# Attention of a fused Mamba, attention and expert layer: short matmul passes joined in pairs, the normalisation of the probabilities shared by VectorE and GpSimd, and the output projection's wait split by batch

## What is computed

```python
x = rmsnorm(hidden_states, ln1_w)                       # (4, 256, 256)
q = (x @ q_w.T).reshape(b, s, 16, 192)[..., :128]        # 16 heads of 128
k = (x @ kv_w.T)[..., :16*128].reshape(b, s, 16, 128)
v = (x @ kv_w.T)[..., 16*128:16*256].reshape(b, s, 16, 128)
scores = einsum('bqnd,bknd->bnqk', q, k) * 192 ** -0.5
scores = where(causal, scores, -1e9)
p = softmax(scores, axis=-1)
attn = einsum('bnqk,bknd->bqnd', p, v).reshape(b, s, 16*128)
hid = hidden_states + attn @ o_w.T
```

## Time and profile before

| | |
|---|---|
| three runs before | 781.72, 781.1, 780.4 us; median 781.1 |
| the profiled execution | 783.59 us |
| its span (first to last instruction) | 781.5 us |
| mean granted TensorE clock | 0.987 |
| busy in the span | PE 744.0 us, PEld 587.5, DVE 574.5, ACT 463.4, POOL 286.6 |
| the attention | from about 266 us to about 550 us of the span |

### The profile page before, as it was taken

One profiled execution on the slowest core, in us unless ns is written; L12 is line 12 of the kernel. 1 busy time (PEld: TensorE's weight loads), 2 busy tenths in 40 slices (PEclk: granted clock), 3 DMA queues, 4 the chain that ended last, 5 costly groups with the idle time before them and its releaser, 6 DMA issues.

```text
span 781.5 us, 12391 instructions
## 1 busy us (share of the span) xinstructions
PE 744.0 (95%) x4164; PEld 587.5 (75%) x4164; DVE 574.5 (74%) x1218; ACT 463.4 (59%) x1022; POOL 286.6 (37%) x181
## 2 busy tenths in 40 slices
PE   7997999999979999999999999999998999999996
PEld 3444455455546899999999999998877888898886
DVE  3699999999898678748775776678665564647376
ACT  4699878878665467727773675476662343425153
POOL 1007989998769711201210211000433231313140
PEclk9998999999999999999999999999999999999999
DMA  8022423333221200000010110001219161515101
GB/s 326 12 75 81 119 97 118 116 103 109 67 77 54 72 28 28 29 28 28 29 55 1 31 50 28 21 21 55 88 53 259 49 179 51 147 50 184 48 0 54
DMA packets 25213, 59.03 MB, mean 76 GB/s; under 512 B 3617, under 2 KB 5153, under 8 KB 25041
## 3 DMA queue, kind: packets, MB, share of 16 engines
q1 hardware_dynamic: 25024, 58.21, 24.3%
q10 hardware_dynamic: 144, 0.26, 0.1%
HBM read 57.21 MB, written 1.25 MB: 75 GB/s over the span
## 4 chain that ended last, share of the span: by engine, by line
PE 58%; DVE 8%; ACT 3%; issue 2%; DMA 1%; DVEq 0%; SPq 0%; ACTq 0%
PE ps L1034 17%; PE ps L1035 17%; PE ps L1036 17%; PE ps L1191 3%; PE ps L549 2%; DVE e_aw L2007 2%; DVE e_sg L1999 1%; ACT e_ah L1853 1%; PE ps L553 1%; DVE e_al L2013 1%; DVE m_ring L903 1%; ACT e_sg L1849 0%; ACT a_p L1343 0%; DVE hid L2018 0%; PE ps L498 0%
## 5 line engine op out<-in xcount | busy, mean ns | idle before, releaser
L549 PE MATMUL ps<-m_ring,ident 128*128 128x512 f32 x256 | 121.7, 604 | 5.6 <-POOL m_ring L406 5.4
L1145 POOL TENSOR_TENSOR a_wl<-raw,a_wh 128x1024 fp32r<-128x1024 f32 (+1 forms) x16 | 32.1, 2008 | 239.4 <-ACT a_wh L1331 239.4
L1668 POOL TENSOR_TENSOR e_wl<-raw,e_wh 128x512 fp32r<-128x512 f32 (+1 forms) x55 | 59.2, 1087 | 154.0 <-ACT e_wh L1804 85.8
L406 POOL TENSOR_TENSOR m_ring<-m_ring,m_c_sb 128x1024 f32<-128x1024 f32 x40 | 94.6, 2373 | 18.3 <-DVE m_ring L903 16.3
L398 POOL TENSOR_TENSOR m_ring<-m_du,m_b_sb 128x1024 f32<-128x1024 f32 x31 | 73.6, 2374 | 59.8 <-DVE m_ring L890 59.8
L549 PEld LDWEIGHTS ps<-m_ring,ident 128*128 128x128 f32 x256 | 47.1, 192 | 50.2 <-issue 37.1
L903 DVE TENSOR_TENSOR_SCAN m_ring<-m_first,ps 128x1024 f32<-128x1024 f32 x32 | 72.8, 2275 | 7.7 <-ACT ps L752 4.2
L1034 PE MATMUL ps<-a_rowsh,e_wh 128*128 128x512 f32 x200 | 78.3, 391 | 0.2 <-ACT e_sg L1849 0.2
L1035 PE MATMUL ps<-a_rowsl,e_wh 128*128 128x512 f32 x200 | 77.9, 389 | 0.0
L1036 PE MATMUL ps<-a_rowsh,e_wl 128*128 128x512 f32 x200 | 77.9, 389 | 0.0
L1343 ACT ACTIVATE a_p<-a_p,a_nmax 128x128 f32<-128x128 f32 (+1 forms) x128 | 57.1, 448 | 29.2 <-DVE a_nmax L1436 27.9
(11 more groups left out here) (221 smaller groups left out, 2144.4 us busy)
## 6 DMA issues: line engine op xcount, KB each, us to landing
raw<-in_expert_w SPq DMA_DIRECT2D x30, 384.0 KB, 3.3
raw<-in_attn_w SPq DMA_DIRECT2D x20, 512.0 KB, 3.3
m_c_sb<-bc SPq DMA_DIRECT2D x40, 256.0 KB, 3.5
m_b_sb<-bc SPq DMA_DIRECT2D x32, 256.0 KB, 4.1
e_wb<-wt SPq DMA_DIRECT2D x18, 256.0 KB, 4.5
e_wb<-wt SPq DMA_DIRECT2D x4, 448.0 KB, 5.8
e_wb<-wt SPq DMA_DIRECT2D x4, 384.0 KB, 4.5
x<-in_x_tok SPq DMA_DIRECT2D x1, 1024.0 KB, 10.2
```

The costliest lines, as they stand in the source:

```text
L406: nc.gpsimd.tensor_tensor(split(slot(n)), split(slot(n)), c_sb[:, k % C_BUFS:k % C_BUFS + 1, :].to_broadcast([P, 2, HALF]), ALU.mult).then ...
L549: nc.tensor.matmul(ps[:, Y_BANK + c, :], ident[:, :], slot(n)[:, c * HALF:(c + 1) * HALF], start=False, stop=False, skip_group_check=True) ...
L1668: nc.gpsimd.tensor_tensor(w[1][:, k, cols], raw[:, k, cols], w[0][:, k, cols].bitcast(F32), ALU.subtract).then_inc(low, 1)
```

## The change

Three things change, and with them two tensors' layouts: the high and low parts of the keys become one tensor `a_k`, those of the transposed probabilities one tensor `a_pT`, so that both parts can stream in one pass.

1. `joined_passes` replaces three passes of 128 columns by one of 128 (low weights by the high streamed part) and one of 256 (high weights by both streamed parts at once). The product with the low streamed part goes to a PSUM block of its own and is added by VectorE: in `maxes` by one more instruction of 128 columns ahead of the others, in `low_o` by one more behind, which waits for the instruction before it (`o_joined`).
2. `normalize` loses its multiplication of 256 columns to GpSimd (a tensor_tensor with the reciprocal broadcast); what stays on VectorE is `one_over`. `turn` waits for both.
3. `outputs(g)` waits for the low parts of each batch in turn instead of for all four.

```diff
@@ Space
-            self.k, self.q, self.rows = (parts(name, [P, 2, T]) for name in ("k", "q", "rows"))
+            self.k = ctx.enter_context(nc.sbuf_tensor("a_k", [P, 2, 2, T], F32R))
+            self.q, self.rows = (parts(name, [P, 2, T]) for name in ("q", "rows"))
...
-            self.pT = parts("pT", [P, 2, 3 * P])
+            self.pT = ctx.enter_context(nc.sbuf_tensor("a_pT", [P, 2, 2, 3 * P], F32R))
@@ new function
+def joined_passes(nc, out, lhs, both, start, stop):
+    lh, ll = lhs
+    nc.tensor.matmul(out[:, 0, :], ll, both[:, 0, :], start=start, stop=False, skip_group_check=True)
+    return nc.tensor.matmul(out, lh, both, start=False, stop=stop, skip_group_check=True)
@@ attention_block, gpsimd
+        def normalize(n, b):
+            pool.wait_ge(rs_done, n + 1)
+            nc.gpsimd.tensor_tensor(p[:, b, P:3 * P], p[:, b, P:3 * P], rs[:, b, 1:2].to_broadcast([P, 2 * P]),
+                                    ALU.mult).then_inc(norm_done, 1)
+
+        def step(g, j, cols):
+            n = g * (GH * BATCH) + j * BATCH
+            for b in range(1, BATCH):
+                normalize(n + b, b)
+            pack(g * GH + (GH + j), j, cols)
+            if not (isinstance(g, int) and g == LAST and j == GH - 1):
+                normalize(n + BATCH, 0)
...
@@ tensor, scores
-            for first, keys, cols in ((t0, P, slice(0, P)), (t0 + P, SEQ, slice(P, 3 * P))):
-                mm = three_passes(nc, bank[:, cols], [x[:, j % 2, first:first + P] for x in q],
-                                  [x[:, j % 2, t0:t0 + keys] for x in k_], first == t0, True)
+            blocks = bank.rearrange("p (a c) -> p a c", c=P)
+            joined_passes(nc, blocks[:, 0:4:3, :], [x[:, j % 2, t0:t0 + P] for x in q],
+                          space.k[:, :, j % 2, t0:t0 + P], True, True)
+            mm = three_passes(nc, bank[:, P:3 * P], [x[:, j % 2, t0 + P:t0 + SEQ] for x in q],
+                              [x[:, j % 2, t0:t0 + SEQ] for x in k_], False, True)
             mm.then_inc(s_ready, 1)
@@ turn
             pe.wait_ge(norm_done, n + 1)
+            pe.wait_ge(first_done, n + 1)
@@ weigh
-            three_passes(nc, bank[:, P:SEQ], vs[1], [x[:, b % 2, 2 * P:3 * P] for x in pT], False,
-                         True).then_inc(o_ready, 1)
+            blocks = bank.rearrange("p (a c) -> p a c", c=P)
+            joined_passes(nc, blocks[:, 1:3, :], vs[1], space.pT[:, :, b % 2, 2 * P:3 * P], False,
+                          True).then_inc(o_ready, 1)
@@ outputs
-            pe.wait_ge(ol_done, g * (GH * BATCH) + GH * BATCH)
             pe.wait_ge(w_done, g * GH + 2 * GH)
             for i in range(TT):
+                if i % 2 == 0:
+                    pe.wait_ge(ol_done, g * (GH * BATCH) + ((GH - 1) * BATCH + i // 2 + 1))
                 pe.wait_ge(r_free, out_unit(g, i) - 1)
@@ vector, maxes
-            nc.vector.memset(rs[:, b, :], 0.0)
-            for t, cols in ((0, slice(0, P)), (1, slice(P, 3 * P))):
-                m = nc.vector.tensor_tensor_reduce(out=p[:, b, cols], in0=ps[:, 2 + b % 2, cols], in1=mask[:, cols],
+            nc.vector.tensor_tensor(p[:, b, 0:P], ps[:, 2 + b % 2, 3 * P:4 * P], mask[:, 0:P], ALU.add
+                                    ).then_inc(masked, 1)
+            for t, cols, more in ((1, slice(P, 3 * P), mask[:, P:3 * P]), (0, slice(0, P), p[:, b, 0:P])):
+                if t == 0:
+
+                    dve.wait_ge(masked, n + 1)
+                    nc.vector.memset(rs[:, b, :], 0.0)
+                m = nc.vector.tensor_tensor_reduce(out=p[:, b, cols], in0=ps[:, 2 + b % 2, cols], in1=more,
@@ normalize, now one_over
             nc.vector.reciprocal(rs[:, b, :], sums[:, b, :]).then_inc(rs_done, 1)
             dve.wait_ge(rs_done, n + 1)
-            for t, cols in ((0, slice(0, P)), (1, slice(P, 3 * P))):
-                m = nc.vector.tensor_scalar(p[:, b, cols], p[:, b, cols], rs[:, b, t:t + 1], None, ALU.mult)
-            m.then_inc(norm_done, 1)
+            nc.vector.tensor_scalar(p[:, b, 0:P], p[:, b, 0:P], rs[:, b, 0:1], None, ALU.mult).then_inc(first_done, 1)
@@ low_o
-                                    ALU.subtract).then_inc(ol_done, 1)
+                                    ALU.subtract).then_inc(o_joined, 1)
+            dve.wait_ge(o_joined, n + 1)
+            late = o[1][:, j, b * SEQ + P:(b + 1) * SEQ]
+            nc.vector.tensor_tensor(late, late.bitcast(F32), ps[:, 6 + b % 2, SEQ:SEQ + P], ALU.add).then_inc(ol_done, 1)
```

More of the change, by code:

```diff
@@ L1048, in attention_block @@
     raw = keep["raw"]
-    w, q, k_, v, p, pT, o = space.w, space.q, space.k, space.v, space.p, space.pT, space.o
+    w, q, v, p, o = space.w, space.q, space.v, space.p, space.o
+    k_, pT = ([x[:, part] for part in range(2)] for x in (space.k, space.pT))
     nmax, sums, rs = (sb(f"a_{n}", [P, 4, 2]) for n in ("nmax", "sums", "rs"))
@@ L1056, in attention_block @@
     rs_done, norm_done = sem("rs_done"), sem("norm_done")
+    masked, o_joined, first_done = sem("masked"), sem("o_joined"), sem("first_done")
     pT_ready, ph_done, pl_done = sem("pT_ready"), sem("ph_done"), sem("pl_done")
@@ L1146, in pack @@
                                     ALU.subtract).then_inc(w_done, 1)
-        with pool.Fori(1, NG) as g:
+        def normalize(n, b):
[9 more added lines that the diff above has]
+                normalize(n + BATCH, 0)
+        normalize(0, 0)
+        for j in range(GH):
+            step(0, j, slice(0, PACK))
+        with pool.Fori(1, LAST) as g:
             for j in range(GH):
-                pack(g * GH + j, j, slice(0, PACK))
+                step(g, j, slice(0, PACK))
         for j in range(GH):
-            pack(NG * GH + j, j, OUT_COLS)
+            step(LAST, j, OUT_COLS)
     def tensor(pe):
@@ L1439, in maxes, with one_over @@
             m.then_inc(max_done, 1)
-        def normalize(n, b):
+        def one_over(n, b):
             dve.wait_ge(exp_done, n + 1)
@@ L1481, in vector @@
             first(s)
-        normalize(0, 0)
+        one_over(0, 0)
         def step(g, j):
@@ L1493, in step @@
             if not units:
-                normalize(n + 1, 1)
+                one_over(n + 1, 1)
                 maxes(n + 2, 2)
@@ L1498, in step @@
                 low_p(n + 1, 1)
-                normalize(n + 2, 2)
-                normalize(n + 3, 3)
+                one_over(n + 2, 2)
+                one_over(n + 3, 3)
                 low_o(n, j, 0)
@@ L1531, in step @@
             low_o(n + 3, j, 3)
-            normalize(n + BATCH, 0)
+            one_over(n + BATCH, 0)
             fill(5)
```

## The result

The changed kernel took 806.9 us (median of 4 runs, 806.1 to 808.09), the kernel before 781.4 (median of 4, 780.4 to 782.23): a ratio of 1.034, interval 1.032 to 1.0361. It is slower, as forecast, but by 25 us and not by 10: the time lies outside the range. It is the time of rival (b).

The account below looks back on a forecast made before the run. Bound twice a step: TensorE 15.26 us, a VectorE-ScalarE chain about 15.16. Chain +0.90, less 0.10 slack and 0.10 shorter weigh 2, gives +0.70 a step; 13 steps 9.1, with the others +10.5: 791.6 us, range 780 to 797.

Parts of the forecast that it names:

- rival (b): GpSimd gets the ports first, VectorE's multiplication waits 0.74 us each time: +1.15 us a step more, 807 us; chance 0.07.
- For batch 2 it helps nothing, since normalize 3 waits for exps 3: VectorE's normalize: losing the 256-column multiplication saves 0 on the chain for batch 2; -0.54 us for batches 1 and 3.
- The slack of 0.10: Chain through VectorE and ScalarE, at weigh 2: it could grow 0.10 us a step before TensorE had to wait.
- the 0.90 of the prediction: Growth of VectorE's chain a step: 0.63 maxes, -0.54 normalize, 0.66 low_o, 0.15 GpSimd's multiplication, +0.90 us.
- `maxes` +0.21: VectorE's maxes: one more addition of 128 columns, +0.21 us, on the chain for batches 0, 2 and 3: +0.63.
- `low_o` 0.67: VectorE's low_o: with the addition behind it 0.67 us instead of 0.34, on the chain for batches 0 and 1: +0.66.
- GpSimd's multiplication: GpSimd's part of normalize: 0.742 us for 256 columns, delaying VectorE's multiplication of batch 3 by 0.15 us.
- The outputs' wait, 0: Start of outputs: TensorE's wait of 0.41 us moves to the second tile, 0 to +0.1 us, not -0.4.
- VectorE's chain, not this, decides when weigh 2 starts: TensorE's turn: probabilities come later, it waits 0.3 us at turn 0 and a like time at turn 2, costing 0.
- Rival (a): TensorE's saving comes through: faster, 778 or 768 us; decided at a chain growth of 0.2 us a step; chance 0.12.
- (c): VectorE's additions are cheaper than the nearest rows or half hidden: growth 0.3 to 0.5 us a step, 783 to 787; chance 0.13.
- (d): No change: the chain's growth and TensorE's saving cancel, 780 to 782.5 us; chance 0.06.

Follow-up runs that it names:

- a1: Changed kernel, but GpSimd's multiplication waits for the end of VectorE's multiplication instead of the reciprocals: 792.1 us.
- a6: Changed kernel, but GpSimd first multiplies two columns of a constant and waits for that, so its 256 columns start later: 790.3 us.
- b1: Kernel before with the split normalisation alone, VectorE's and GpSimd's multiplications both waiting for the reciprocals: 788.3 us.
- b3: Kernel before with the scores' passes joined alone, and the addition in maxes that this needs: 789.2 us.
- a2: Changed kernel with the whole normalisation back on VectorE; joined passes and split outputs' wait stay: 797.3 us.
- b2: Kernel before with the outputs' wait split by batch, alone: 781.2 us, ratio 1.002.
- c6: Scores joined for batch 1, weigh for 2 and 3; GpSimd helps batches 1 and 3, after VectorE; outputs by batch: 776.2 us, 0.9933 of the kernel before.
- a4: Changed kernel with GpSimd's multiplication of 256 columns cut into two instructions of 128: 793.1 us.
- a5: Changed kernel with VectorE's multiplication over 127 columns instead of 128, one column left unnormalised: 806.7 us.

## Why the prediction was right in its direction and wrong in its size

The step that failed is this sentence: "VectorE saw its own after 0.04 us; GpSimd should take a little longer, so VectorE goes first and GpSimd waits for its 0.28." GpSimd was recorded 0.05 us after VectorE and it was VectorE that waited. I had set the delays of two semaphores, one of them unknown, against each other, though the earlier trace rows showed only that the order decides, and gave the other order 0.07. With no row for GpSimd's delay the two orders deserved nearly even chances. That the step failed is shown by a1 and a6, which change only when GpSimd starts and come out at 15.97 and 15.95 us, the forecast being 15.96. The last sign named in the prediction, a multiplication of 0.7 us or more everywhere, is what came: all of the 64 last 0.74 but the program's first two.

What the failed step cost, term by term on the chain: the rows of the changed kernel, and in brackets those of the same step of a1, where VectorE goes first:
- batch 0: fill 5's low part starts 5.13 us into the step (4.95), +0.18. In a1 it waits for ScalarE's high part; in the changed kernel it starts at 402.92, 0.17 behind the 402.75 at which that part would allow it;
- batch 1: `one_over` holds 0.84 (0.39), +0.45;
- batch 2: its `one_over` holds 0.85, so that VectorE comes 0.21 behind the end of exps 3 (0.02), and from one `one_over` to the next it takes 0.85 (0.66), +0.19. The prediction had "For batch 2 it helps nothing, since normalize 3 waits for exps 3", which is right for a gain; that it also had no room for a loss was overlooked, in rival (b) too;
- batch 3: 0.85, 409.42 to 410.27 (0.51), +0.34.

Together 1.16 by these rows of one step, each rounded; 17.10 less 15.97 is 1.13. The 402.75 comes from ScalarE's row

```profile
402.14 0.58 ACT L1368 ACTIVATE a_vh<-ps 128x512 fp32r<-128x512 f32 x1
```

(402.72, and about 0.03 for the semaphore). These four are read off the rows; no run varied one alone.

Two more terms were off, and they cancel. The slack of 0.10 was not there: before, `weigh` 2 starts 0.07 us behind the end of `low_p` 2, and where TensorE does wait for it it starts 0.05 to 0.06 behind. b1 and b3, which lengthen the chain by 0.57 each, cost 0.57 and 0.58 a step. And the chain grew by less than the 0.90 of the prediction: in a1 `low_p` 2 begins 13.25 us into the step (404.81) instead of 12.45 (402.21), +0.80, half of the difference being batch 3's 0.51 for 0.55 and the rest 0.01 in each addition. 0.80 less 0.10 for the shorter `weigh` 2 is the 0.70; 0.90 less 0.20 was the same number.

The other steps:
- TensorE's saving of 0.10 a join: right (0.59 for 0.69).
- `maxes` +0.21: right. The changed kernel's VectorE starts `maxes` 0 at 399.23 and `maxes` 1 at 399.99, 0.76 for 0.55:

```profile
399.23 0.28 DVE L1467 TENSOR_TENSOR a_p<-ps,mask 128x128 f32<-128x128 f32 x1
...
399.99 0.29 DVE L1467 TENSOR_TENSOR a_p<-ps,mask 128x128 f32<-128x128 f32 x1
```

- `low_o` 0.67: it is 0.66 (401.40 to 402.06). The joins as a whole: +1.13 in a2, against the 1.09 expected there.
- GpSimd's multiplication: 0.61, not the 0.742 of the nearest row, whose two inputs are both full tensors. Where GpSimd is second (a1) this lies beside VectorE's work; in the changed kernel it is the length of the hold.
- The outputs' wait, 0: right, and for the reason given (b2). After, the second tile waits 1.10 for fill 5's low part (the row at 420.75).
- "VectorE's chain, not this, decides when weigh 2 starts": right; the waits for GpSimd are 6.3 us in all, against 28.4 for `low_p`.
- The sum over the steps: +10.5 forecast, +11.1 measured for the attention of a1 (293.70 less 282.57). Its parts: steps inside a group 10 x 0.70 = 7.0, three boundaries 0.71, 0.73 and 0.62, the first step +0.95 (0.5 forecast), the last but one +0.36 (0.2), the last +0.75 (0.7). For the changed kernel: 10 x 1.84, boundaries 1.39, 1.40 and 1.30, first +1.27, last but one +1.28, last +1.08: 26.1.

Rival (a) fell with the first row: growth was far above its 0.2, and so did (c) and (d): even in a1 the chain grows by 0.80. Rival (b) happened, at 806.9 us for its 807, but in part by a cancellation: its GpSimd instruction was too long (0.74 for 0.61) and its batch 2 was missing.

## What to carry to other kernels

An engine that is 80% busy can still be a second bound, here with next to nothing to spare: follow one period through every engine and write down the slack before costing a change that saves on the busiest one. If a neighbour that shares the ports takes over work, don't let both start on the same semaphore; make the one on the critical chain go first (here one wait, worth 15 us), because losing the ports cost more than the work handed over. And add the extra instructions of such a join only for those batches where they stand beside the chain: eight joins alone cost 1.13 us a step (a2), three well-placed ones, with GpSimd's ordered help, gained 0.40 (c6).

## What the hardware showed that was not expected

- An earlier record does not mean the ports. VectorE's multiplication is recorded 0.04 or 0.05 us before GpSimd's (402.25 and 402.30), and it is the one that is held, until GpSimd's end. The turning point is close: with GpSimd's 0.08 to 0.10 later (batch 3 in a4) VectorE isn't held, nor with 0.32 (a6). Nor is it in the program's first multiplication, with 0.05 (b1) or 0.06 (a5 and the changed kernel), so that the recorded starts, to 0.01 us, don't tell the order for certain. The changed kernel's first, VectorE's and then GpSimd's (its next instruction is merged into the row):

```profile
272.04 0.29 DVE L1483 TENSOR_SCALAR a_p<-a_p,a_rs 128x128 f32<-128x128 f32 x1
```

```profile
272.10 1.28 POOL L1162 TENSOR_TENSOR a_p<-a_p,a_rs 128x256 f32<-128x256 f32 x2 [3.45 <-DVE a_rs L1481]
```

  (The Trainium skill, "SBUF — State Buffer", section "SBUF: two separate sides", gives the ports to whichever starts first; by the recorded starts the trace doesn't agree where GpSimd's comes 0.04 or 0.05 us later, 62 times of 64, and does from 0.08 us on.)
- The hold is one instruction of GpSimd long: 0.74 against 256 columns (0.61), 0.53 against 128 (0.40).
- GpSimd's multiplication by a broadcast column is 0.61 us for 256 columns and 0.40 for 128; that of two full tensors of 2 columns is 0.19 (a6).
- The attention begins between 263.0 and 267.3 us in profiles of kernels whose earlier part is the same. So the two profiled spans differ by 22.6 us (804.1 less 781.5) where the attention differs by 26.1 and the medians by 25.5. For changes as small as b2, the length of the changed part is the better measure.
